# Edge features kept transposed in a graph network kernel: TensorE takes the means of their layer norm, and the gathers of a chunk signal in four groups

## The reference

```python
for i in range(3):
    q = (h @ Wq[i]).reshape(n, 4, 16);  k = ...;  v = ...
    scores = jnp.einsum('ehd,ehd->eh', q[dst], k[src]) / 4
    scores = scores + e @ We[i]
    p = jnp.exp(scores - segment_max(scores, dst)[dst])
    alpha = p / (segment_sum(p, dst)[dst] + 1e-09)
    agg = segment_sum((alpha[:, :, None] * v[src]).reshape(-1, 64), dst)
    h = _ln(h + agg @ Wo[i], gn[i], bn[i])
    emsg = gelu(concatenate([h[src], h[dst], e]) @ Wem[i] + bem[i])   # tanh form
    e = _ln(e + emsg, ge[i], be[i])      # over 32 features; the last e is not used
# _ln: (x - mean) / sqrt(var + 1e-05) * g + b
```

## Time and profile before

| | us |
|---|---|
| three runs | 13641.84, 13666.16 (median), 13691.0 |
| the profiled execution | 13628.23 |
| its span in the profile | 13626.5 |
| mean granted clock of TensorE | 0.517 of full speed |
| busy: POOL | 9350.4 (69%) |
| busy: DVE | 5502.6 (40%) |
| busy: ACT | 2945.4 (22%) |
| busy: PE | 1874.4 (14%) |

### The profile page before, as it was taken

The page is one execution under the profiler, slowest core; times in us unless marked ns, Lnnn a source line. Parts: engine busy times, 40 slices in busy tenths (PEclk is TensorE's granted clock), DMA queues, the critical chain, the costliest instruction groups (busy, mean ns, idle before and its releaser), DMA issues. The chain is left out here.

```text
span 13626.5 us, 53780 instructions
## 1 busy us (share of the span) xinstructions
PE 1874.4 (14%) x8861; PEld 1678.3 (12%) x8861; DVE 5502.6 (40%) x9285; ACT 2945.4 (22%) x3341; POOL 9350.4 (69%) x8816
## 2 busy tenths in 40 slices
PE   5434220010001000000100010001110322232222
PEld 4333210000000000000000010001010221121111
DVE  5333232222222222222222235443544477747776
ACT  0010021111111111111111112221222244424442
POOL 4888867767776776777677757776665576646664
PEclk7555555555555555555555555555555555555555
DMA  4333322212221221122132223332332343323332
GB/s 156 34 36 34 27 73 48 50 36 49 50 49 34 50 50 45 40 50 49 36 89 82 86 66 114 105 100 80 106 105 89 94 138 126 128 79 130 129 119 74
DMA packets 586154, 1033.50 MB, mean 76 GB/s; under 512 B 313972, under 2 KB 378456, under 8 KB 574840
## 3 DMA queue, kind: packets, MB, share of 16 engines
q0 software_dynamic: 394720, 416.04, 16.7%
q1 hardware_dynamic: 139542, 306.39, 6.5%
q10 hardware_dynamic: 51842, 310.55, 5.7%
HBM read 615.16 MB, written 430.03 MB: 77 GB/s over the span
## 5 line engine op out<-in xcount | busy, mean ns | idle before, releaser
L753 POOL DMA_INDIRECT turned<-d_t,idx x7056 | 7174.7, 1017 | 2842.5 <-issue 2424.7
L935 DVE COPY idx<-src 128x28 int32 x252 | 46.2, 183 | 4785.9 <-DMA turned<-d_t,idx 4692.7
L608 POOL DMA_INDIRECT d_acc<-sums,idx x784 | 1234.2, 1574 | 267.9 <-issue 235.3
L823 ACT COPY wide<-wide 128x1848 f32<-128x1848 f32 (+1 forms) x252 | 922.9, 3662 | 1614.7 <-issue 868.2
L808 ACT ACTIVATE banks<-factors 128x28 f32<-128x28 f32 (+1 forms) x252 | 55.7, 221 | 4902.3 <-issue 3900.7
L1018 DVE TENSOR_TENSOR_SCAN wide<-banks,wide 128x224 f32<-128x224 f32 (+1 forms) x1008 | 1024.1, 1079 | 5.8
L1343 PE MATMUL banks<-ident,tail 128*65 128x128 f32 (+1 forms) x9 | 4.1, 460 | 6675.9 <-issue 4409.7
L1002 DVE TENSOR_TENSOR wide<-turned,banks 128x1792 f32<-128x1792 f32 x252 | 843.7, 3348 | 0.0
L1343 PEld LDWEIGHTS banks<-ident,tail 128*65 128x65 f32 (+1 forms) x9 | 1.5, 167 | 6678.0 <-issue 4410.5
L843 PE MATMUL banks<-ident,wide 128*128 128x128 f32 x994 | 283.7, 433 | 3052.7 <-issue 1205.7
L918 DVE TENSOR_TENSOR_SCAN wide<-banks,wide 128x448 f32<-128x448 f32 (+1 forms) x725 | 624.2, 901 | 61.9 <-issue 33.9
(11 more groups left out here) (272 smaller groups left out, 6336.6 us busy)
## 6 DMA issues: line engine op xcount, KB each, us to landing
d_e<-wide ACTq DMA_DIRECT2D x168, 924.0 KB
turned<-d_t,idx POOLq DMA_INDIRECT x7056
d_e<-wide ACTq DMA_DIRECT2D x84, 1008.0 KB
wide<-d_b SPq DMA_DIRECT2D x60, 1344.0 KB
wide<-d_b SPq DMA_DIRECT2D x60, 896.0 KB
wide<-d_edge SPq DMA_DIRECT2D x86, 448.0 KB
d_b<-wide SPq DMA_DIRECT2D x28, 1344.0 KB
b_rows<-d_b SPq DMA_DIRECT2D x29, 896.0 KB
```

Of the source, the lines that this page charges most:

```text
L608: gp.indirect_dma_start(g.d_acc[r][:, :], offset(idx[:, b, k:k + 1]), sums[:, b, k, :], None, compute_op=ALU.add).then_inc(added[b][r], 16)
L753: gp.indirect_dma_start(rows[:, b, k, :], None, table[:, :], offset(idx[:, b, k:k + 1])).then_inc(s["gathered"][b], 16)
L823: nc.scalar.copy(state[:, b], values[:, b].rearrange("p f k -> p k f")).then_inc(s["states_turned"], 1)
```

## The change

Edge features are held transposed throughout (32 features of 4 edges on the 128 partitions, `e_T`), and `d_eT` in memory takes the place of `d_edge`. The first multi pass turns the given features once, as before, and stores them turned. In an update chunk TensorE accumulates the pre-activation in PSUM: `w_em` times the old features, plus the ends' sum brought in by a product with the identity. ScalarE takes gelu from there. TensorE subtracts the mean by a product with the matrix `centre` (identity minus `mean`), once over the old features and once over the message; ScalarE squares; TensorE takes the mean of the squares with `mean`; ScalarE forms the inverse root as exp(-0.5 ln(var + 1e-5)); VectorE multiplies the two (`scale_edges`), and ScalarE applies scale and shift. All this goes in two halves, of 512 and 384 columns. Each chunk's gathers signal in four groups of seven, and VectorE works through them group by group, sums of ends and score products in turn. The index list is written after them. The copy of features in the dot pass is gone.

```diff
+            link(nc.vector.tensor_scalar(g.mean[:], group[:, 0:P], group[:, P:], 1.0 / DE, ALU.is_equal, ALU.mult))
+            link(nc.vector.tensor_tensor(g.centre[:], g.ident[:], g.mean[:], ALU.subtract))
...
+                if update:
+                    sp.wait_ge(s["e_stored"][b], 16 * (t + 1))
+                    sp.dma_start(e_T[:, b], g.d_eT[bass.ds(chunk * P, P), :]).then_inc(s["e_loaded"][b], 16)
+                elif multi:
+                    sp.dma_start(e_rows[:, b], edge_rows(a["edge_pad"])[:, cols, :]).then_inc(s["e_loaded"][b], 16)
...
-                if kind == "dot":
-                    sp.dma_start(edge_rows(g.d_edge)[:, cols, :],
-                                 edge_rows(a["edge_pad"])[:, cols, :]).then_inc(s["e_stored"][b], 16)
...
-                                          offset(idx[:, b, k:k + 1])).then_inc(s["gathered"][b], 16)
+                                          offset(idx[:, b, k:k + 1])).then_inc(gathered[k // LINE][b], 16)
...
+        def turn_e(chunk, b, round_):
+            act.wait_ge(s["e_stored"][b], 16 * (round_ + 1))
+            for half, (x0, x1) in enumerate(PARTS_OF):
+                act.wait_ge(s["e_turned"], 2 * chunk + half + 1)
+                nc.scalar.copy(e_T[:, b, x0:x1], ps_a[:, x0:x1]).then_inc(s["e_copied"], 1)
+        def store_e(chunk, b):
+            act.dma_start(g.d_eT[bass.ds(chunk * P, P), :], e_T[:, b]).then_inc(s["e_stored"][b], 16)
...
-                    act.wait_ge(s["pre_ready"], chunk + 1)
-                    nc.scalar.activation(flat(pre[:]), flat(pre[:]), ACT.Gelu_apprx_tanh).then_inc(s["gelu_done"], 1)
...
-                    act.dma_start(edge_rows(g.d_edge)[:, cols, :], e_rows[:, b]).then_inc(s["e_stored"][b], 16)
+                    for half, (x0, x1) in enumerate(PARTS_OF):
+                        act.wait_ge(s["pre_done"], 2 * chunk + half + 3)
+                        nc.scalar.activation(emsg[:, x0:x1], ps_a[:, x0:x1],
+                                             ACT.Gelu_apprx_tanh).then_inc(s["gelu_done"], 1)
+                    for half, (x0, x1) in enumerate(PARTS_OF):
+                        act.wait_ge(s["centred"], 2 * chunk + half + 1)
+                        nc.scalar.activation(sq[:, x0:x1], ps_b[:, x0:x1], ACT.Square).then_inc(s["squared"], 1)
+                    for half, (x0, x1) in enumerate(PARTS_OF):
+                        act.wait_ge(s["var_done"], 2 * chunk + half + 1)
+                        nc.scalar.activation(rstd[:, x0:x1], ps_a[:, x0:x1], ACT.Ln,
+                                             bias=eps[:, 0:1]).then_inc(s["logged"], 1)
+                    for half, (x0, x1) in enumerate(PARTS_OF):
+                        act.wait_ge(s["logged"], 2 * chunk + half + 1)
+                        nc.scalar.activation(rstd[:, x0:x1], rstd[:, x0:x1], ACT.Exp,
+                                             scale=-0.5).then_inc(s["rooted"], 1)
+                    for half, (x0, x1) in enumerate(PARTS_OF):
+                        act.wait_ge(s["scaled"], 2 * chunk + half + 3)
+                        nc.scalar.activation(e_T[:, b, x0:x1], unit[:, x0:x1], ACT.Identity, bias=gs[:, 1:2],
+                                             scale=gs[:, 0:1]).then_inc(s["e_ready"], 1)
...
-                if update:
-                    turn_e(2 * chunk + 2)
+                if multi:
+                    act.wait_ge(s["e_ready" if update else "e_copied"], 2 * chunk + (2 if update else 4))
+                    store_e(chunk, b)
...
+        def before_norm(chunk, b, round_):
+            pe.wait_ge(s["e_loaded"][b], 16 * (round_ + 1))
+            pe.wait_ge(s["scaled"], 2 * chunk + 2)
             for half, (q0, q1) in enumerate(HALVES):
-                if half:
-                    pe.wait_ge(s["e_copied"], 2 * n + 1)
+                x0, x1 = PARTS_OF[half]
+                nc.tensor.matmul(ps_a[:, x0:x1], w_em[:], e_T[:, b, x0:x1], start=True, stop=False)
                 for q in range(q0, q1):
-                    mm = nc.tensor.transpose(ps_eT[:, (q - q0) * P:(q - q0 + 1) * P],
-                                             e_columns(b, q), g.ident[:])
+                    pe.wait_ge(s["ends_summed"], 4 * chunk + (4 * q + 3) // LINE + 1)
+                    mm = nc.tensor.matmul(ps_a[:, q * P:(q + 1) * P], ends[:, q * P:(q + 1) * P], g.ident[:],
+                                          start=False, stop=q == q1 - 1)
+                mm.then_inc(s["pre_done"], 1)
+        def norm(chunk, b):
+            pe.wait_ge(s["we_read"], chunk + 1)
+            for half, (x0, x1) in enumerate(PARTS_OF):
+                nc.tensor.matmul(ps_b[:, x0:x1], g.centre[:], e_T[:, b, x0:x1], start=True, stop=False)
+                pe.wait_ge(s["gelu_done"], 2 * chunk + half + 1)
+                nc.tensor.matmul(ps_b[:, x0:x1], g.centre[:], emsg[:, x0:x1],
+                                 start=False, stop=True).then_inc(s["centred"], 1)
+            for half, (x0, x1) in enumerate(PARTS_OF):
+                pe.wait_ge(s["squared"], 2 * chunk + half + 1)
+                nc.tensor.matmul(ps_a[:, x0:x1], g.mean[:], sq[:, x0:x1], start=True,
+                                 stop=True).then_inc(s["var_done"], 1)
...
-        def old_product(chunk, b, round_, again=True):
-            pe.wait_ge(s["e_loaded"][b], 16 * (round_ + 1))
...
-            mm.then_inc(s["e_product"], 1)
...
                 if update:
-                    pe.wait_ge(s["e_product"], chunk + 1)
-                    pe.wait_ge(s["e_ready"][b], t + 1)
-                    turn(2 * chunk + 1, b)
+                    before_norm(chunk, b, t)
+                    norm(chunk, b)
+                    pe.wait_ge(s["e_ready"], 2 * (chunk + 1))
                 else:
-                    pe.wait_ge(s["e_loaded"][b], 16 * (t + 1))
-                    turn(chunk, b)
+                    turn(chunk, b, t)
+                    pe.wait_ge(s["e_copied"], 2 * chunk + 4)
                 pe.wait_ge(s["we_read"], chunk + 1)
                 for q in range(G4):
-                    if q % 4 == 0:
-                        pe.wait_ge(s["e_copied"], 2 * (turns * chunk + turns - 1) + q // 4 + 1)
-                    mm = nc.tensor.matmul(ps_we[:, q * 16:(q + 1) * 16], e_T[:, q, :], w_e[:],
+                    mm = nc.tensor.matmul(ps_we[:, q * 16:(q + 1) * 16], e_T[:, b, q * P:(q + 1) * P], w_e[:],
                                           start=True, stop=True)
                 mm.then_inc(s["we_product"], 1)
-                if update:
-                    old_product(chunk + 1, 1 - b, t + b)
...
-                v.wait_ge(s["gathered"][b], 16 * K * (t + 1))
-                nc.vector.tensor_copy(idx[:, b], g.src[:, bass.ds((chunk + 2) * K, K)]).then_inc(s["idx_ready"][b], 1)
...
-                    nc.vector.tensor_tensor(e, pre[:], mid(gs[:, 1], K), ALU.add).then_inc(s["e_ready"][b], 1)
+                def landed(i):
+                    v.wait_ge(gathered[i][b], 16 * LINE * (t + 1))
+                def next_idx():
+                    nc.vector.tensor_copy(idx[:, b], g.src[:, bass.ds((chunk + 2) * K, K)]).then_inc(s["idx_ready"][b], 1)
+                def scale_edges(half):
+                    x0, x1 = PARTS_OF[half]
+                    v.wait_ge(s["rooted"], 2 * chunk + half + 1)
+                    nc.vector.tensor_tensor(unit[:, x0:x1], ps_b[:, x0:x1], rstd[:, x0:x1],
+                                            ALU.mult).then_inc(s["scaled"], 1)
...
-                    for q0, q1 in LINES:
+                    if update:
+                        v.wait_ge(s["pre_done"], 2 * chunk + 2)
+                    for i, (q0, q1) in enumerate(LINES):
+                        landed(i)
+                        if update:
+                            nc.vector.tensor_tensor(ends[:, q0 * DE:q1 * DE].rearrange("p (k f) -> p k f", f=DE),
+                                                    G[:, q0:q1, 0:DE], B[:, q0:q1, D:D + DE],
+                                                    ALU.add).then_inc(s["ends_summed"], 1)
                         last = nc.vector.tensor_tensor(prod[:, q0:q1], G[:, q0:q1, k0:k0 + D], B[:, q0:q1, 0:D], ALU.mult)
                     link(last)
+                    next_idx()
...
+                if update:
+                    scale_edges(0)
+                    for i in range(3):
+                        spread_next(i)
+                    scale_edges(1)
+                    for i in range(3, PARTS):
+                        spread_next(i)
...
-                if kind != "gat":
-                    for i in range(PARTS - 1 if update else 0, PARTS):
+                if kind != "gat" and not update:
+                    for i in range(PARTS):
                         spread_next(i)
```

132 lines of the change are left out of this document (53 added, 79 removed).

## The result

The changed kernel takes 13,739.25 us (median of 15 runs, 13,663.44 to 13,827.95), the one before 13,659.85 (15 runs beside it, 13,637.83 to 13,692.36). The ratio is 1.0057, with an interval of 1.0035 to 1.008: 79 us slower. The forecast was 13,790, slower by 125. The spread of the changed kernel's runs has trebled, 164 us against 54. Its profiled execution is one of the fastest of the fifteen, 13,663.94 us (span 13,662.2); against the profiled execution before it is only 36 us longer.

A forecast was written before the change was run, and what follows sets the result against it. Gather issue was taken to set the pace, with late TensorE products costing the update passes 465 us. 118 - 33 - 20 + 60 = +125 us gave a median of 13,790; likeliest range 13,700 to 13,890, whole 13,390 to 14,010.

The forecast's parts named there:

- The chain: Update chunks: the norm over TensorE and ScalarE makes a chunk 38.3 us for 36.2, +2.1, over 56 chunks +118 us.
- 118 - 33 = +85: Update passes: +118 us for the norm's chain, -33 for starting when a group of seven gathers has landed.
- the two waits that the forecast put at 10.1 + 0.6 us a chunk: VectorE in update chunks: 10.1 us ahead of the first scaling, then from 25.6 to 26.2 for the product with w_e.
- The held products: Update passes: TensorE results reaching readers late, 465 us before; taken as +60 us, with ends of -465 and +465.
- The other passes: First chunks, dot and first multi pass: earlier starts by groups and a dropped copy of features, together -20 us.
- the signs named for being right: Update chunks: VectorE idle 10 us ahead of L980, about 26 us from first sum to L1016; passes of 1260 to 1290.
- Not held any more: Rival, update passes: TensorE's products no longer late, -285 us, median 13,380; half gone, 13,535; chance 0.32 for both.
- The rival's floor of 39.2 us a chunk: Update passes: gathers alone cost 39.2 us a chunk, so a pass takes 1098 us instead of 1222 and 1239.
- Held more: Rival, update passes: delayed chunks caught at their first TensorE result, +10 us in every second chunk, +345, median 14,010; chance 0.12.
- No growth: Rival, update passes: the chain's 2 us vanish beside the gather stream, leaving -20 to +40, near 13,680; chance 0.16.
- The rule of the Trainium skill that was weighed: Update passes: by it gathers never reach TensorE's products, so the +60 falls away and the sum is +65 us.
- The second rule: ScalarE's table loads: one set for exp and ln would save one load of three a chunk, 72 us; not counted on.

The follow-up runs named there:

- the seventh experiment: Changed kernel with 16 instead of 28 gathers a chunk in the update passes and 12 GpSimd memsets replacing the others: one run of 12,210 us, passes 993 and 989.
- condition B: Later runs, graph attention pass 978 to 990 us: changed kernel 12,220.58 us, kernel before 12,447.86 beside it, ratio 0.982.
- condition A: Earlier runs, graph attention pass 1070 us, as in both first profiles: changed kernel 13,739.25 us, kernel before 13,659.85, ratio 1.0057.
- The pair with 16 gathers: Update passes with 16 of 28 gathers a chunk: kernel before, 988 and 988 us; changed kernel with memsets replacing the other 12, 993 and 989.
- the first experiment: Changed kernel with 16 instead of 28 gathers in each update-pass chunk: ratio 0.9711 to the kernel before, passes of 1009 and 1019 us.
- experiment 4: Changed kernel with VectorE waiting for all four groups of gathers before the first sum: ratio 1.0123, then 1.0040, to the kernel before.
- 6: Changed kernel with the update passes' product with w_e as two products with w_e as weights, result unused: ratio 0.9793 to the kernel before.

## Why the prediction came out right, and where it didn't

**The chain.** The forecast put the first scaling at 18.0 us and the product's end at 26.2 us into a chunk. In the chunk shown 17.6 and 26.1 were measured, and that is luck: the pre-activation was complete 9.0 us in, for 6.4, and the centrings and means took 5.3 us (12887.78 to 12893.12), for 9.1, at a granted clock of 0.83 where the forecast had priced them by rows at 0.50. With nothing held (the seventh experiment) the first scaling comes 15.4 us in, the read 24.0, and a chunk takes 35.6 us, for 18.0, 26.2 and 38.3. So the norm's chain, +2.1 us a chunk and +118 in the sum, was mis-sized, and TensorE's part of it most of all. VectorE's busy time fell by 407 us, where 8.1 us a chunk, 454, were forecast. The sum over both update passes: -407 busy, +473 waits of the chain with nothing held, -69 other waits. That makes -3, where the forecast had 118 - 33 = +85. The 473 come from a run in condition B; in A no run is free of late results, but the changed kernel's first scaling comes 14.3 us in at the earliest there, so the chain isn't longer in A. The pair with 16 gathers, both in B, one with memsets on GpSimd, says +6. Either way the new chain costs next to nothing, and the two waits that the forecast put at 10.1 + 0.6 us a chunk, 599 in all, and that are 584 in the first experiment, are 111 us of late results and 473 of chain.

**The held products** carry the loss: forecast +60, measured 1023 - 473 = 550 after and 465 before, +85 in the profiled execution. With the -3 that is +82, and the passes' lengths say +82. Twice as many results of TensorE are in VectorE's way, and the loss grew by a fifth. The experiments show that it isn't a price per result: a pause in the stream, or the read moved forward, shifts the held time from one result to another and leaves 512 to 741 us of it. The end of the stream bounds it, as the forecast had it, but nearly half of the late reads come free before. Chunks held in the norm for 28.9 us and more came five times in the first update pass of the profiled run, which is 54 us longer than the second with its one; that their number makes the spread of the runs is likely, but one trace doesn't show it. The median lies 75 us above it.

**The other passes.** -20 was forecast, 36 - 82 = -46 came in the profiled execution, of which 18 in the first multi pass, whose products are held as well and vary by as much (experiment 4). The rest is spread over the program. The forecast had named more than 30 us here as a sign of its being wrong.

**The total.** +36 in the profiled execution, +79 in the medians, +125 forecast. That the size fits is luck in good part: 85 us were forecast for the norm and the groups, and nothing was found; 60 for held results, and 85 were found. Counted from the profiled execution the total would be 13,702, at the lower end of the range, and why the median lies above it no trace shows. The direction is right in condition A only, the condition of the profile from which the forecast was made, and it rests on the held results. Of the signs named for being right, VectorE's wait ahead of the scaling is there (9.3 and 9.7 us in the median, but up to 33.1); the read comes 33.5 and 34.3 us after the first sum of ends in the median, not 26; and the passes of 1298 and 1244 us lie on either side of 1260 to 1290. Two slips of the working: the terms of the range give 13,730 to 13,916 and not 13,700 to 13,890, and L980 was waited for 11 times in the second pass, not 8 or 9.

**The rivals.** "Not held any more" gave 13,380, 285 us faster, with VectorE below the gathers' floor. In condition A it didn't come. In B nothing is held in either kernel, so its sum, which takes the old kernel's held time as the gain, has no case there; the 227 us come, as far as the traces show, from GpSimd's shorter gathers and from pauses that are gone. The rival's floor of 39.2 us a chunk was wrong as a constant: it moves with VectorE's work and with the condition. "Held more" put the held results at +280 more and not at 25; its waits on ScalarE are there, but rare (16.9 and 20.4 us ahead of Gelu). "No growth", near 13,680, is nearer to the profiled execution (13,702 counted as above) than the forecast is, and a little further from the median of 13,739 (59 us for 51). The total alone doesn't decide between the two. What that rival let vanish beside the stream, 2 us of chain a chunk, wasn't there to begin with.

The rule of the Trainium skill that was weighed (SBUF — State Buffer, "SBUF: two separate sides": engine ports and DMA ports never contend, TensorE never waits on anyone) would have had no result late beside gathers. In condition A they are up to 23 us late there, in B none is; whether a port of SBUF has to do with it no run shows. The same section has GpSimd and VectorE share a port that one of them can lock, among others by an operation of VectorE with two inputs in SBUF. The trace agrees as to which operations lengthen a gather, 1.76 us beside L971 for 0.95. The second rule, one table for Ln and Exp (ScalarE: Activation LUTs, "Table sets: the hidden batching unit"), wasn't tried. The chunk shown spends two loads of tables in the chain of the norm, 1.28 us each by the earlier trace rows, and only the second of them follows the variance without cover.

## What stays open

What delays TensorE's results: the gathers' descriptors, their data, or a third thing that condition A brings and that shows only beside gathers; and what frees them while gathers go on. Whether the loss in condition A is 79 us because of the held results alone: the sum above is of one execution, with a chain measured in B. Why the graph attention passes take 1070 us at one time and 978 to 990 at another, with the same median distance of 1.25 us between gathers and only a tenth of them longer. Whether loads of weights are what is held. The two runs made for this (6 and 7) met condition B, where there was nothing to see.

## What to carry to other kernels

Work taken off a busy engine and replaced by a chain over three engines, with nothing of that engine's own work beside it, is not yet a gain: here 7.3 us of VectorE's work a chunk were bought with 8.4 us of its waiting when nothing was held. It paid where another engine, GpSimd, was the bound and got faster by it. Look at what else runs while an engine waits before you shorten the chain: 6 us less chain gained nothing where the results came late beside GpSimd's stream. Take the length of a chain from a run in which nothing disturbs it: the disturbed one agreed with the forecast by luck. And run a change of half a per cent beside the old kernel in more than one session: this one is 0.6% slower in one condition and 1.8% faster in the other, each within a quarter of a per cent.

## What the runs showed that I hadn't expected

- Results of TensorE that had run reached their readers up to 23 us late (13279.74 to 13303.17) beside GpSimd's gathers in condition A: 3.3 to 3.7 us after these stopped in the two chunks shown, but 22 of 48 late reads while they went on. In B the same kernel's read waited 1.0 us throughout.
- The same kernel on the same chip took 13,605 us in one set of runs and 12,473 in the next; a graph attention pass of it takes 1069 us in the first profile and 990 in the one of condition B.
- In condition B a gather's issue on GpSimd took 0.95 us beside an idle VectorE and beside its scans, and 1.76 on average beside a product of two operands in SBUF.
- TensorE's granted clock over an update pass rose from 0.52-0.53 to 0.58-0.61; in the chunk shown it was at 0.83 while products of 512 and 384 columns followed one another.
